# Attention FM on one core: a three-slot PSUM ring, longer bursts of one kind of matmul, paced gathers and a table copied by DMA

## The chip, the cores and the metric

One of the eight cores of a Trainium2 chip runs the kernel. The metric is the device time of one execution in microseconds. The three runs of the kernel before took 919.03, 920.51 and 921.53 us, median 920.51.

## What is computed

For 2048 samples of 32 fields, with a table of 12500 rows of 64 values:

```python
V = emb_v[x]                                   # 32 x 2048 x 64
iu, ju = np.triu_indices(32, k=1)              # the 496 pairs of fields
VV = V[iu] * V[ju]
hid = relu(einsum('pbk,kh->pbh', VV, at_w) + at_b)
score = einsum('pbh,ho->pbo', hid, at_h)
pooled = sum(VV * score, axis=0)
prob = sigmoid(pooled @ p + w0 + sum(w1[x], axis=0))
```

Everything is fp32.

## The kernel before, in words

The batch is worked off in 32 fills (`FILLS`) of 64 samples. A fill has two groups g of 16 samples side by side in columns, and two halves of the partitions, 64 embedding values each. A middle fill t goes through these stages.

Gather (GpSimd, L218 to L235): 16 indirect DMAs, each 128 rows of a table into `rows`. `rows` has two buffers; the first two fills read `emb_v` itself, later ones a joint table in HBM that holds the w1 value beside each row, once before it and once behind it, in two copies. The table is built at the start: SP loads `emb_v` and w1 (L191 to L195), VectorE and ScalarE copy them together (`join`, L329 and L380), SP stores four pieces (L202). Before each fill's gathers an index copy, `idx_stage` (L221), is made. GpSimd starts on fill t as soon as the rows of fill t-2 have been turned and their w1 values kept (L246, L247).

Turn (TensorE, L444 to L457): eight transposes of `rows` into the PSUM tile `TR`. ScalarE copies `TR` to `V` (L369) and, multiplied by p, to `pV` (L376), and the w1 values to `w1_all` (`w_all` in the profile, L392).

Products (VectorE, L336 to L351): 16 rounds a fill, one for each pair of step s (8 of them) and group g. A round is two tensor_tensor operations that write 1024 columns of pair products into one of eight slots of `X`.

Hidden (TensorE, L466 to L478): for each round four fp32 matmuls of 64x64 weights by 512 columns, which are eight matmul instructions in the profile, into `Z`, a ring of two slots of two PSUM banks each. ScalarE applies bias and ReLU to 1024 columns and writes one of eight slots of `H` (L424). TensorE waits at L471 for the ReLU of two rounds earlier.

Scores (TensorE, L488 to L501): `score_w` by `H`, 32-column weights in four column groups at a time, 16 matmul instructions a step, accumulated in `S`. `clear_scores` (L480 to L486) opens the accumulation with four bf16 matmuls on zeros.

Grams (TensorE, L503 to L520): for each of 16 samples and each g a matmul of 64-column weights from `pV` by 32 columns of `V` into `G`, so 64 matmul instructions a fill, in four quarters.

Pair sums (VectorE, L313 to L327): `gram` is `G` under a mask, `prod` is `S` times `gram`, `part` is its sum; done for fill t-1 in rounds 4 to 6 of fill t.

The order on TensorE is written out by hand in `products` (L528 to L546): after which of the 16 rounds scores, grams and turn come. It is, for one fill: rounds 0 and 1, scores of steps 6 and 7 of the fill before, rounds 2 and 3, a quarter of the grams, rounds 4 and 5, a quarter, rounds 6 and 7, clearing and scores of steps 0 and 1, round 8, turn of the next fill, round 9, scores of steps 2 and 3, rounds 10 and 11, a quarter, rounds 12 and 13, a quarter, rounds 14 and 15, scores of steps 4 and 5. The linear term (L548 to L561), 32 small matmuls, stands behind round 10 of the last fill. Fills 1 to 30 run in a hardware loop with two fills in its body.

## Time and profile before

| | us |
|---|---|
| three runs, median | 920.51 |
| the profiled execution, its own time | 918.6 |
| its span, from the first to the last instruction | 916.8 |
| TensorE busy | 866.9 |
| VectorE busy | 708.2 |
| ScalarE busy | 675.2 |
| GpSimd busy | 563.4 |

The profile is of one execution. The span is cut into instructions by line; "idle before" a group is time in which its engine had nothing to run, and what ended it. PE is TensorE's matmuls, PEld its weight loads, DVE VectorE, ACT ScalarE, POOL GpSimd, SP the queue of plain DMAs. The chain follows what ended last backwards through what each instruction waited for.

### The profile page before, as it was taken

The numbers are of one execution on the slowest core, as the hardware profiler recorded it, in microseconds if no ns is written. First come the engines' busy times: TensorE is split into PE (matmuls) and PEld (weight loads), VectorE is DVE, ScalarE is ACT, GpSimd is POOL, SyncE is SP. The second block draws the span as 40 slices with busy tenths as digits, with TensorE's granted clock in tenths as the row PEclk, the third lists the DMA queues.
The fourth block names the chain that finished last, engine by engine and source line by source line (L and its number), as shares of the span: only waits on it lengthen the run. The fifth ranks groups of instructions, "written<-read, shape, count | busy, mean of one in ns | idle before, by whom it ended". The sixth has DMA issues, their size and how long they took to land.

```text
span 916.8 us, 27050 instructions
## 1 busy us (share of the span) xinstructions
PE 866.9 (95%) x10676; PEld 339.1 (37%) x10676; DVE 708.2 (77%) x1179; ACT 675.2 (74%) x771; POOL 563.4 (61%) x584
## 2 busy tenths in 40 slices
PE   0549999999999999999999999999999999999998
PEld 0113333333433333333333333333333333333333
DVE  3555789777778977777898777779877777987772
ACT  3327777787877778787777788777778877777884
POOL 5717767555566765565676556556665555666770
PEclk9878999999999999999999999999999999999999
DMA  8972222222222222222222222222222222222000
GB/s 169 174 143 25 25 26 21 19 19 19 18 21 22 22 19 19 19 19 20 22 23 19 19 19 19 20 21 22 21 19 19 19 19 20 23 19 20 8 1 2
DMA packets 19638, 27.35 MB, mean 30 GB/s; under 512 B 10646, under 2 KB 10662, under 8 KB 18982
## 3 DMA queue, kind: packets, MB, share of 16 engines
q0 software_dynamic: 17408, 17.07, 25.0%
q1 hardware_dynamic: 1566, 10.02, 2.8%
q8 instruction: 11, 0.18, 0.1%
q10 hardware_dynamic: 648, 0.03, 0.0%
q14 instruction: 5, 0.04, 0.0%
HBM read 20.59 MB, written 6.51 MB: 30 GB/s over the span
## 4 chain that ended last, share of the span: by engine, by line
PE 92%; POOL 4%; DMA 2%; issue 1%; DVE 0%; SPq 0%; ACT 0%; POOLq 0%; DVEq 0%
PE Z L476 53%; PE S L497 26%; PE G L515 8%; PE TR L455 4%; POOL rows L233 3%; DMA rows<-in_L_rec_emb_v_dram,idx_stage 2%; PE S L485 1%; PE TR L556 0%; DMA idx_raw<-in_r_x_dram 0%; SPq L188 0%; ACT y_sb L439 0%; DVE prod L323 0%; DVE part L326 0%; POOL idx_stage L221 0%; PE TR L566 0%
## 5 line engine op out<-in xcount | busy, mean ns | idle before, releaser
L424 ACT ACTIVATE H<-Z,bias 128x1024 f32<-128x1024 f32 x512 | 546.5, 1112 | 192.2 <-PE Z L476 191.2
L348 DVE TENSOR_TENSOR X<-V 128x992 f32<-128x992 f32 (+15 forms) x1024 | 640.2, 696 | 24.2 <-ACT V L369 20.8
L233 POOL DMA_INDIRECT rows<-table,idx_stage x480 | 489.2, 1019 | 167.4 <-issue 144.5
L476 PE MATMUL Z<-X,w_sb 64*64 64x512 f32 x4096 | 517.2, 608 | 1.5 <-DVE X L348 1.2
L497 PE MATMUL S<-H,score_w 128*32 128x496 f32 (+15 forms) x4096 | 248.3, 383 | 0.0
L476 PEld LDWEIGHTS Z<-X,w_sb 64*64 64x64 f32 x4096 | 123.7, 131 | 182.4 <-issue 174.8
L497 PEld LDWEIGHTS S<-H,score_w 128*32 128x32 f32 x4096 | 111.2, 110 | 184.4 <-issue 139.8
L323 DVE TENSOR_TENSOR prod<-S,gram 128x512 f32<-128x512 f32 x32 | 22.1, 692 | 159.0 <-PE S L497 159.0
L515 PEld LDWEIGHTS G<-V,pV 128*64 128x64 f32 x2048 | 70.0, 137 | 103.8 <-issue 103.8
L221 POOL COPY idx_stage<-idx 128x16 uint32 (+1 forms) x32 | 7.1, 222 | 143.5 <-ACT w_all L392 122.6
L376 ACT ACTIVATE pV<-TR,pcol 64x512 f32<-64x512 f32 x128 | 87.0, 680 | 2.5
L515 PE MATMUL G<-V,pV 128*64 128x32 f32 x2048 | 84.3, 225 | 0.0
L455 PE MATMUL TR<-ident,rows 128*128 128x128 f32 x256 | 36.9, 289 | 44.6 <-DMA rows<-in_L_rec_emb_v_dram,idx_stage 44.6
L455 PEld LDWEIGHTS TR<-ident,rows 128*128 128x128 f32 x256 | 28.7, 146 | 70.6 <-issue 63.0
L369 ACT COPY V<-TR 128x512 f32<-128x512 f32 x64 | 34.2, 587 | 24.5 <-PE TR L455 24.5
L242 POOL DMA_INDIRECT w_all<-in_L_rec_w_dram,idx x32 | 33.5, 1048 | 9.8 <-issue 9.8
L233 POOL DMA_INDIRECT rows<-in_L_rec_emb_v_dram,idx_stage x32 | 32.7, 1023 | 10.8 <-issue 9.2
L317 DVE TENSOR_TENSOR gram<-G,upper 128x512 f32<-128x512 f32 x32 | 21.8, 681 | 8.1 <-PE G L515 8.1
L326 DVE TENSOR_REDUCE part<-prod 128x512 f32 (+1 forms) x32 | 21.8, 680 | 0.0
L485 PEld LDWEIGHTS S<-zeros 128*32 128x32 bf16 x128 | 3.3, 92 | 26.0 <-issue 26.0
L485 PE MATMUL S<-zeros 128*32 128x512 bf16 x128 | 12.8, 390 | 0.0
L392 ACT COPY w_all<-rows 128x8 f32 x60 | 9.3, 202 | 0.7
(38 smaller groups left out, 42.6 us busy)
## 6 DMA issues: line engine op xcount, KB each, us to landing
rows<-table,idx_stage POOLq DMA_INDIRECT x480
table<-joined SPq DMA_DIRECT2D x2, 1592.5 KB
table<-joined SPq DMA_DIRECT2D x2, 1560.0 KB
raw<-in_L_rec_emb_v_dram SPq DMA_DIRECT2D x1, 3104.0 KB, 11.7
rows<-in_L_rec_emb_v_dram,idx_stage POOLq DMA_INDIRECT x32, 12.3
w_all<-in_L_rec_w_dram,idx POOLq DMA_INDIRECT x32
idx_raw<-in_r_x_dram SPq DMA_DIRECT2D x4, 64.0 KB, 2.2
raw_w<-in_L_rec_w_dram SPq DMA_DIRECT2D x1, 48.5 KB, 13.4
```

What stands on the lines that cost most here:

```text
L233: pool.indirect_dma_start(out=rows[parity][:, g * FILL_M + m, half, c0:c1], out_offset=None, in_=source[half] if joint else source, in_off ...
L242: pool.indirect_dma_start(out=w1_all[:, Q, n:n + 1], out_offset=None, in_=w1, in_offset=at).then_inc(w1_first, 16)
L323: nc.vector.tensor_tensor(prod[:, :, :], S[:, :, :], gram[:, :, :], ALU.mult).then_inc(prod_ready, 1)
L348: last_one = nc.vector.tensor_tensor(xo, vj, vi.unsqueeze(3).to_broadcast(shape), ALU.mult)
L369: nc.scalar.copy(V[parity][:, g, :, :], TR[:, g, :].rearrange("p (b f) -> p b f", f=FIELDS)).then_inc(v_ready, 1)
L376: nc.scalar.activation(pV[parity][k, g, :, half, :, :], TR[k, g, :].rearrange("p (b i c) -> p b c i", c=2, i=FIELDS // 2), ACT.Copy, scale ...
L424: nc.scalar.activation(H[:, r % H_SLOTS, :, :], Z[:, r % Z_SLOTS, :, :], ACT.Relu, bias=bias[:, 0:1]).then_inc(hid_ready, 1)
L455: last = nc.tensor.transpose(TR[:, g, 128 * m:128 * m + 128], embs[:, g * FILL_M + m, 1:1 + 2 * EMB], ident[:, :])
L476: last = nc.tensor.matmul(Z[64 * par:64 * par + 64, r % Z_SLOTS, half, :], w_sb[k, :], X[k, r % X_SLOTS, par, :], start=True, stop=True)
L485: nc.tensor.matmul(S[32 * Q:32 * Q + 32, :, :], zeros[:, 0:32], zeros[:, :].rearrange("p (b j) -> p b j", j=FIELDS), start=True, stop=False)
L497: last = nc.tensor.matmul(S[at:at + 32, :, j0:FIELDS], score_w[:, slot, :], hid.rearrange("p (b j) -> p b j", j=nj), start=False, stop=(s ...
L515: last = nc.tensor.matmul(G[64 * g:64 * g + 64, b, :], pV[parity][:, g, b, :, :, :].rearrange("p h c i -> p (h c i)"), V[parity][:, g, b, ...
```

## The change

TensorE's order becomes four rounds and then scores, four times a fill. The turn of the next fill stands between the scores behind round 7 and round 8, all grams of the next fill behind the scores of round 15. Step and group now alternate in `ORDER`.

`Z` gets a third slot. `TR` is gone: the turn writes into the slot of the ring that would be next (`TURN_SLOT`), and the rounds behind it go on with the slot after it, so that rounds 8 and 9 wait for the ReLU of two rounds earlier and all others of three; round 10 waits for the copy of `V`. `S` and `G` are gone too: a tile `SG` for each parity holds the grams, which VectorE takes out under the mask, and then the scores, the first of which opens the accumulation; the clearing is dropped. A gram matmul of 64 columns becomes two of 32, in four column groups, 128 matmul instructions a fill. `pV` is one buffer, filled from `V` instead of `TR` with two masks of p, so its zeros need no memset. `V` is copied in one operation of 1024 columns.

GpSimd reads its indices straight from `idx`, or for the joint table from `joint_idx` (VectorE computes 66 times the index, plus 0 or 1), since there is now one table of 66 values a row, read from value 0 or 1 on as a flat list. Three fills read `emb_v` itself. The loop over fills is unrolled. The 16 gathers of a fill are in four groups of four, each released when TensorE has done a certain round: round 15 of the fill three before, and rounds 3, 7 and 11 of the fill two before. Of the 48 gathers of w1 one follows each fill, the rest come last.

SP loads `emb_v` only when the rows of fill 0 have landed, in 13 DMAs that write straight between the w1 columns; GpSimd writes those (`joined[:, :, :, c]`). `join` is gone. For the first fill the turn goes through `SG`. The linear term moves behind the last scores, in four row groups.

The diff, cut to what the text speaks of ("..." marks what is left out):

```diff
-ORDER = [(s, g) for four in (0, 4) for g in range(2) for s in range(four, four + 4)]
-SCORED_AFTER = {7: (0, 1), 9: (2, 3), 15: (4, 5)}
-LAST_STEPS, LAST_AFTER = (6, 7), 1
-GRAMS_AFTER = (3, 5, 11, 13)
-BATCHES = 4
-X_SLOTS, Z_SLOTS, H_SLOTS = 8, 2, 8
+ORDER = [(s, g) for s in range(STEPS) for g in range(2)]
+FIRST_ORDER = [(s, g) for g in range(2) for s in range(STEPS // 2)] + ORDER[ROUNDS // 2:]
+TURN_BEFORE = 8
+SCORED_AFTER = {3: (-1, (6, 7)), 7: (0, (0, 1)), 11: (0, (2, 3)), 15: (0, (4, 5))}
+LAST_STEPS = (6, 7)
...
+X_SLOTS, H_SLOTS, Z_SLOTS = 4, 4, 3
...
+JOINT = EMB + 2
+RUN = 8
+PLAIN_FILLS = 3
+PACE, PACED_FROM, PACED_EVERY = 2, 16, 4
...
+def z_slot(r):
+    return (r if r < TURN_BEFORE else r + 1) % Z_SLOTS
+TURN_SLOT = TURN_BEFORE % Z_SLOTS
+def z_before(r):
+    if r == 2:
+        return -3
+    if r < 2:
+        return r - 2
+    return r - 2 if TURN_BEFORE <= r < TURN_BEFORE + 2 else r - 3
...
-        S = ps("S", [128, GROUP, FIELDS])
-        G = ps("G", [128, GROUP, FIELDS])
-        TR = ps("TR", [128, 2, COLS])
-        logit = TR[0:QUARTERS, 0, :]
+        SG = [ps(f"SG{i}", [128, GROUP, FIELDS]) for i in range(2)]
...
+            for g in range(2):
+                sp.wait_ge(first_rows[g], 16 * GATHERS // 2)
+            sp.dma_start(tail[:, :, 1:1 + EMB], last_rows[0]).then_inc(tail_loaded, 16)
+            for k, (c0, c1) in enumerate(HALF_CHUNKS):
+                for c in range(c0, c1):
+                    sp.dma_start(joined[:, c, :, 1:1 + EMB], chunks(emb_v, c, c + 1)[:, 0, :, :]).then_inc(joined_loaded[k], 16)
+            sp.wait_ge(w1_joined, 4)
+            sp.wait_ge(tail_loaded, 16)
+            sp.dma_start(last_rows[1], tail[:, :, :]).then_inc(table_stored, 16)
+            for k, (c0, c1) in enumerate(HALF_CHUNKS):
+                sp.wait_ge(joined_loaded[k], 16 * (c1 - c0))
+                sp.dma_start(chunks(table, c0, c1), joined[:, c0:c1, :, :]).then_inc(table_stored, 16)
...
+            flat = table.rearrange("v (k o) -> (v k) o", o=1)
+            def gather(t, paced=False):
+                joint = t >= PLAIN_FILLS
+                source, at_rows = (flat, joint_idx) if joint else (emb_v, idx)
                 for g in range(2):
                     for m in range(FILL_M):
+                        if paced and m % PACE == 0:
+                            pool.wait_ge(z_ready, ROUNDS * (t - 3) + PACED_FROM + PACED_EVERY * (FILL_M * g + m) // PACE)
...
+            for half in range(2):
+                nc.gpsimd.memset(rows[0][:, :, half, W1_AT[half]], 0.0).then_inc(w1_cleared, 1)
+            pool.wait_ge(idx_ready, 1)
+            gather(0)
+            pool.wait_ge(w1_loaded, 32)
+            for c in (0, 1 + EMB):
+                nc.gpsimd.tensor_copy(joined[:, :, :, c], raw_w1[:, :, :]).then_inc(w1_joined, 1)
+                nc.gpsimd.tensor_copy(tail[:, :, c], tail_w1[:, :]).then_inc(w1_joined, 1)
+            pool.wait_ge(idx_ready, 2)
+            gather(1)
+            pool.wait_ge(first_turned, 2)
+            gather(2)
+            pool.wait_ge(rows_turned, 1)
+            pool.wait_ge(idx_ready, 4)
+            pool.wait_ge(table_stored, 16 * 3)
+            gather(3)
+            for t in range(4, FILLS):
+                pool.wait_ge(rows_turned, t - 2)
                 pool.wait_ge(w1_kept, 2 * (t - 3))
-                gather(t, parity, table)
-            pool.wait_ge(idx_ready, 1)
-            gather(0, 0, emb_v)
-            pool.wait_ge(idx_ready, 2)
-            gather(1, 1, emb_v)
-            pool.wait_ge(rows_turned, 2)
-            for half in range(2):
-                pool.wait_ge(table_stored[half], 16 * (1 + len(JOINS)))
-            gather(2, 0, table)
-            pool.wait_ge(rows_turned, 4)
-            gather(3, 1, table)
-            with pool.Fori(4, FILLS - 1, 2) as t:
-                refill(t, 0)
-                refill(t + 1, 1)
-            gather_w1(0)
-            gather_w1(1)
+                gather(t, paced=True)
+                gather_w1(1)
+            gather_w1(PLAIN_FILLS * GATHERS)
...
+            def mask_gram(t, parity):
+                dve.wait_ge(gram_ready, t + 1)
+                shape = [128, GROUP, FIELDS - 1]
+                nc.vector.tensor_tensor(gram[parity][:, :, 1:FIELDS], SG[parity][:, :, 1:FIELDS],
+                                        upper[:, 1:FIELDS].unsqueeze(1).to_broadcast(shape), ALU.mult
+                                        ).then_inc(gram_masked, 1)
+            def weigh(t, parity):
+                dve.wait_ge(gram_masked, t + 1)
+                dve.wait_ge(scored, STEPS * (t + 1))
+                nc.vector.tensor_tensor(prod[:, :, 1:FIELDS], SG[parity][:, :, 1:FIELDS], gram[parity][:, :, 1:FIELDS],
+                                        ALU.mult).then_inc(prod_ready, 1)
...
+                for r, (s, g) in enumerate(FIRST_ORDER if first else ORDER):
+                    if first and r in (0, STEPS // 2):
+                        dve.wait_ge(first_v, g + 1)
+                    if r == 8:
+                        mask_gram(t, parity)
+                    if r == 10 and not first:
+                        weigh(t - 1, 1 - parity)
+                    if r == 12 and not first:
+                        sum_pairs(t - 1)
+                    if not first:
+                        dve.wait_ge(z_ready, ROUNDS * t + r - 2 * X_SLOTS + 1)
...
+            def keep_v(t, parity):
+                act.wait_ge(rows_turned, t)
+                if not (isinstance(t, int) and t == 1):
                     act.wait_ge(x_ready, ROUNDS * (t - 1))
                     act.wait_ge(gram_ready, t - 1)
-                nc.scalar.copy(V[parity][:, g, :, :], TR[:, g, :].rearrange("p (b f) -> p b f", f=FIELDS)
+                nc.scalar.copy(V[parity][:, :, :], Z[:, TURN_SLOT, :, :].rearrange("p g (b f) -> p (g b) f", f=FIELDS)
                                ).then_inc(v_ready, 1)
-            def keep_pv(parity, g):
+            def keep_pv(t, parity, half):
+                if isinstance(t, int) and t == 0:
+                    act.wait_ge(first_v, 2)
+                    act.wait_ge(pmask_ready, 1)
+                else:
+                    act.wait_ge(v_ready, t)
+                    act.wait_ge(gram_ready, t)
...
+                nc.scalar.activation(pV[:, :, half, :, :], V[parity][:, :, :].rearrange("p b (i c) -> p b c i", c=2),
+                                     ACT.Copy, scale=pmask[:, half:half + 1]).then_inc(pv_ready, 1)
...
+                    if not last and not first:
+                        if r == 8:
+                            keep_v(t + 1, 1 - parity)
+                        if r == 10:
+                            keep_pv(t + 1, 1 - parity, 0)
+                        if r == 12:
+                            keep_w1(t + 1, 1 - parity)
+                        if r == 14:
+                            keep_pv(t + 1, 1 - parity, 1)
...
+                if r == TURN_BEFORE + 2 and not first and not last:
+                    pe.wait_ge(v_ready, t + 1)
+                elif not first or r >= Z_SLOTS:
+                    pe.wait_ge(hid_ready, ROUNDS * t + z_before(r) + 1)
...
+            def grams(t, parity):
+                pe.wait_ge(pv_ready, 2 * t + 2)
+                if not (isinstance(t, int) and t <= 1):
+                    pe.wait_ge(prod_ready, t - 1)
+                for b in range(GROUP):
                     for g in range(2):
-                        last = nc.tensor.matmul(G[64 * g:64 * g + 64, b, :],
-                                                pV[parity][:, g, b, :, :, :].rearrange("p h c i -> p (h c i)"),
-                                                V[parity][:, g, b, :], start=(b == 0), stop=(b == GROUP - 1),
-                                                skip_group_check=True)
+                        for half in range(2):
+                            at = 32 * (2 * g + half)
+                            last = nc.tensor.matmul(SG[parity][at:at + 32, b, :],
+                                                    pV[:, g * GROUP + b, half, :, :].rearrange("p c i -> p (c i)"),
+                                                    V[parity][:, g * GROUP + b, :], start=(b == 0), stop=(b == GROUP - 1),
+                                                    skip_group_check=True)
+                last.then_inc(gram_ready, 1)
...
+                    if r == TURN_BEFORE and not first and not last:
+                        pe.wait_ge(hid_ready, ROUNDS * t + TURN_BEFORE - Z_SLOTS + 1)
+                        turn(t + 1, 1 - parity)
+                    hidden(t, r, first, last)
                     if first and r == 3:
-                        turn(0, 0, (1,))
-                        keep_busy(8)
-                    if r == 8 and not last:
-                        pe.wait_ge(pv_ready, 4 * t + 4)
-                        turn(t + 1, 1 - parity)
+                        first_turn(1)
+                    if first and r == 5:
+                        grams(0, 0)
+                    if first and r == ROUNDS - 1:
+                        pe.wait_ge(hid_ready, ROUNDS - 2)
+                        turn(1, 1)
                     if r in SCORED_AFTER:
-                        if r == min(SCORED_AFTER):
-                            clear_scores(t, first)
-                        scores(t, SCORED_AFTER[r])
-                    if r == 10 and last:
-                        linear_term()
-                    if r == LAST_AFTER and not first:
-                        scores(t - 1, LAST_STEPS)
-                    if r in GRAMS_AFTER:
-                        grams(t, parity, first, r)
+                        back, steps = SCORED_AFTER[r]
+                        for s in steps:
+                            if back == 0:
+                                scores(t, parity, s)
+                            elif not first:
+                                scores(t - 1, 1 - parity, s)
+                    if r == ROUNDS - 1 and not last:
+                        grams(t + 1, 1 - parity)
...
+                for Q in range(QUARTERS):
+                    for q in range(QUARTERS):
+                        rng = slice(32 * q, 32 * q + 32)
+                        nc.tensor.matmul(logit[:, q, :], pick[rng, QUARTERS - 1 - Q:2 * QUARTERS - 1 - Q],
+                                         w1_all[rng, Q, :], start=(Q == 0), stop=False,
+                                         tile_position=(32 * q, 0), skip_group_check=True)
+            over_fills(pe, products)
+            for s in LAST_STEPS:
+                scores(FILLS - 1, (FILLS - 1) % 2, s)
+            linear_term()
```

## Rows read from the trace of the kernel before

**Rows 1.** The page, busy us by engine with share of the span and instructions.

```profile
PE 866.9 (95%) x10676; PEld 339.1 (37%) x10676; DVE 708.2 (77%) x1179; ACT 675.2 (74%) x771; POOL 563.4 (61%) x584
```

**Rows 2.** Windows: length, busy us (instructions) of PE, PEld, DVE, ACT, POOL, clock, DMA.

```profile
93.52:891.92 798.40, 798.40 (x9964) 311.72 (x9968) 649.91 (x1052) 625.24 (x721) 506.01 (x520) 1.00 0.24 19
```

**Rows 3.** The chain of waits through one fill: start us, length us, line, instructions.

```profile
522.44 1.02 PE TR L455 x8
523.46 1.02 PE Z L476 x8
524.48 1.86 PE S L497 x32
526.34 1.88 PE Z L476 x16
528.22 0.59 PE G L515 x16
...
538.89 2.07 PE Z L476 x16
...
545.94 0.33 PE S L485 x4
546.27 1.76 PE S L497 x32
```

**Rows 4.** Timeline of ScalarE and VectorE in that fill: start us, length us.

```profile
527.51 2.12 ACT L424 ACTIVATE H<-Z,bias 128x1024 f32<-128x1024 f32 x2 [1.83 <-PE Z L476]
...
534.50 2.80 ACT L376 ACTIVATE pV<-TR,pcol 64x512 f32<-64x512 f32 x4
537.32 0.31 ACT L392 COPY w_all<-rows 128x8 f32 x2
...
538.96 0.69 DVE L323 TENSOR_TENSOR prod<-S,gram 128x512 f32<-128x512 f32 x1 [4.96 <-PE S L497]
```

**Rows 5.** Timeline of TensorE's weight loads.

```profile
516.74 0.55 PEld L515 LDWEIGHTS G<-V,pV 128*64 128x64 f32 x16 [0.81 <-issue]
...
892.91 0.18 PEld L497 LDWEIGHTS S<-H,score_w 128*32 128x32 f32 x12 [0.30 <-issue]
```

**Rows 6.** The page: the gathers, two DMAs by their landing, the gathers' queue.

```profile
q0 software_dynamic: 17408, 17.07, 25.0%
...
L233 POOL DMA_INDIRECT rows<-table,idx_stage x480 | 489.2, 1019 | 167.4 <-issue 144.5
...
raw<-in_L_rec_emb_v_dram SPq DMA_DIRECT2D x1, 3104.0 KB, 11.7
...
rows<-in_L_rec_emb_v_dram,idx_stage POOLq DMA_INDIRECT x32, 12.3
```

**Rows 7.** Timeline of GpSimd at the head of a fill's gathers.

```profile
540.02 1.41 POOL L233 DMA_INDIRECT rows<-table,idx_stage  x1 [0.30 <-issue]
541.73 1.43 POOL L233 DMA_INDIRECT rows<-table,idx_stage  x1 [0.30 <-issue]
```

**Rows 8.** Timeline of the start.

```profile
24.84 1.09 PE L455 MATMUL TR<-ident,rows 128*128 128x128 f32 x4 [24.84 <-DMA rows<-in_L_rec_emb_v_dram,idx_stage]
...
28.91 4.95 DVE L348 TENSOR_TENSOR X<-V 128x992 f32<-128x992 f32 x8
...
41.81 1.12 PE L455 MATMUL TR<-ident,rows 128*128 128x128 f32 x4 [6.71 <-DMA rows<-in_L_rec_emb_v_dram,idx_stage]
```

**Rows 9.** The chain of waits through the start.

```profile
2.10 2.54 DMA idx_raw<-in_r_x_dram
...
48.47 18.83 DMA rows<-in_L_rec_emb_v_dram,idx_stage
...
96.63 1.02 PE TR L455 x8
```

**Rows 10.** The chain of waits through the end.

```profile
898.76 3.59 PE TR L556 x32
...
908.35 3.63 PE S L497 x64
```

331 lines of the change are left out of this document (136 added, 195 removed).

## The prediction

> **What bounds the kernel now.** I read the page's busy times first, then windows by stage, then the chain of waits through one fill, then the timelines of the loads, of ScalarE, VectorE and GpSimd, and last the two ends. TensorE is busy 95% of the span [rows 1]. The windows show where it is not: 798.40 us with TensorE busy throughout, between a start of 93.5 us and an end of 24.9 us (916.8 - 891.92) [rows 2]. The middle is 30 fills, 891.92 - 93.52 = 798.4, so 26.61 us each. There VectorE is busy 649.91 / 30 = 21.7 us a fill, ScalarE 625.24 / 30 = 20.8 and GpSimd 506.01 / 30 = 16.9, the issue ahead of its gathers not counted. Only work taken from TensorE's own line shortens the middle.
>
> One fill, from the chain [rows 3]: seven pairs of rounds at 1.88 us (13.16) and two single rounds at 1.02 (2.04), 0.37 of extra in three of the pairs, the longest 2.07, four S groups of two steps at 1.86 (7.44), the clearing 0.23 (0.33, less the 0.10 by which the S group behind it is shorter), four G quarters at 0.59 (2.36), TR 1.02. Sum 26.62. A round that continues a burst costs 1.88 - 1.02 = 0.86, one that begins a burst 1.02: each change to another kind of matmul and back costs 0.16 in Z alone. There are nine such excursions a fill.
>
> **The change, part by part, in a middle fill.**
> Rounds. The order of work becomes: four rounds, S, four rounds, S and TR, four rounds, S, four rounds, S and G. A burst of four is 1.02 + 3 x 0.86 = 3.60, four of them 14.40, against 15.20 + 0.37: -1.17. The 0.37 goes if the third slot removes the wait for ScalarE. Check: ScalarE does a ReLU every 1.01 us inside a pair (two in 2.12, each 1.11) [rows 4], slower than 0.86, so it falls behind in a burst and catches up under S. Over rounds 8 to 15 TensorE has 1.02 + 3.60 + 1.86 + 3.60 + 1.86 + 1.25 = 13.2 us. ScalarE has 8 x 1.01, one V copy of 1024 columns (as a ReLU, 1.11), two pV copies of 1024 columns (0.68 for 512 now; 1.2 each taken, bounds 1.11 and 1.36) and 0.3 for w_all: 11.9 [rows 4]. Laid out in order, the first ReLU 1.24 us behind the start of its round, each round finds its slot free; the closest is round 15, which needs the ReLU of round 12, about 0.2 us earlier. Round 10 needs the V copy, 0.5 us early. So nothing is charged, and what is late next is that round 15.
> Clearing: -0.23. S stays 7.44.
> G. 64 matmul instructions with 64-column weights, two column groups at a time, become 128 with 32-column weights, four at a time. Now 16 loads take 0.55, one 0.14, so a pair follows a pair after (0.55 - 0.14) / 7 = 0.059. In S, which loads the 32-column form that G will have, twelve loads (three fours, with only 16 columns moving in the ones between) lie within 0.18, one taking 0.11: (0.18 - 0.11) / 2 = 0.035 from four to four [rows 5]. 32 fours x 0.035 + 0.13 for the change of mode = 1.25, against 2.36: -1.11. Bounds: below, the loads inside a four are some 0.01 apart in all, which leaves 0.030, and no change of mode behind S: 1.0. Above, every instruction keeps today's share, 0.59 / 16 = 0.037, 128 x 0.037 = 4.7. I take the S rows, which have the same shape.
> TR stays 1.02; it now sits directly behind S.
> Sum: 14.40 + 7.44 + 1.02 + 1.25 = 24.11 us a fill, 2.51 less.
>
> **What the others need in 24.11.** VectorE: the same products, three pair operations of 31/32 the size: 21.7. Its wait for S before prod, 4.96 us [rows 4], shrinks to about 2.4, and its products stay up to eight rounds ahead. The gram mask waits for the G at the end of the fill before; VectorE gets there within 0.3 us of it. ScalarE: 20.5. GpSimd: 17 gathers (16 and one of w1) at 1.02 [rows 6] and 0.31 of issue [rows 7] = 22.6; the idx_stage copy goes. The groups are released four rounds apart (6.0 us for 4 x 1.33 = 5.3) and the last one is due 13 rounds after its release, so the rows are there in time. Nobody waits for a paced gather; what is queued behind the pacing wait is only the next gather.
>
> **The start.** Now the first rows are turned at 24.84, the second half at 41.81 [rows 8], fill 1's at 67.3, fill 2's at 96.63 [rows 9]. Fill 1's gathers were issued from 28.6 to 48.5 and the last landed 18.83 us later, beside table loads and stores. After: gathers start about 1 us earlier (the copy at L221 and the issue behind it go); eight at 1.25 end at 15.6, and with no table on the queues landing is 2.5 us, as for idx_raw [rows 9]; turned at 18. The second eight: 25.6, turned at 28. GpSimd's line then sets much: w1 copies about 1, gather(1) to 47.9, gather(2) to 69.1, gather(3) to 90. Moving the table behind the first rows puts its 3.1 MB load into 28 to 50 or so and its store behind it. Bounds: the plain load landed in 11.7 us [rows 6]; by the gathers' cost, 25.0% of 16 x 916.8 us over 544 gathers of 128 rows, nearly all of 256 or 260 bytes, 0.053 us a row, 12500 rows take 41. At 25 the table is stored by 69, when gather(3) wants it. On SP's queue the loads, one per chunk, stand behind the wait for the first rows; behind them is only the output. The joins leave VectorE and ScalarE, which the first products waited behind (28.91 against a turn at 24.84 [rows 8]).
> Fill 1's rows land 2.5 to 12.3 us after 47.9 [rows 6, 9]; I take 7: 55. Then TR 1.02, V 1.11, pV 2.4, G 1.25, and 2 x 3.60 + 2 x 1.86: 16.7, so fill 2 is turned at 71.7. GpSimd allows 69.1 + 2.5 = 71.6. With 12.3 it is 77. I take 74, against 96.63 now. That is 22.6 us.
>
> **The end.** From the turn point of the last fill: 2 x 3.60 + 3 x 1.86 = 12.8, then 4.8 as now (912.0 to 916.8) [rows 10]. The linear term, 3.59 of the chain now, stands behind the last S and beside 1.4 us of VectorE (prod at 0.69 [rows 4] and its sum, as long); in four row groups it is 0.9 (bound 3.59, then 2.2 us show). Its remaining 20 w1 gathers, 25 us, have about 45 us.
>
> **Sum.** 74 + 30 x 24.11 + 12.8 + 4.8 = 814.9 of span. The profiled execution took 918.6 at a span of 916.8: +1.8 = 816.7. The median of 920.51 is 1.9 above it: 818.6, so **818 us**.
>
> **Rivals.**
> A. *G does not run four wide.* With pairs at 0.059, 64 x 0.059 + 0.13 = 3.9 a fill, +2.65 x 30: 898. For: no row has more than twelve such loads in a row, and the 128 now come in one block. Against: the S rows. 0.07. By the upper bound, 4.7 and 922, nothing is gained: 0.02.
> The Trainium skill (TensorE: Matmul & The Clock Gate, "Wait — 56ns, not 53.3ns?") says that the starts of matmuls never come closer than about 25 ns; by that G would be 128 x 0.025 = 3.2 us and the kernel about 876 (an estimate from the page). Twelve loads of S within 0.18 us, each 0.11 long and followed by its matmul, speak against it here.
> B. *GpSimd becomes the bound, and the kernel is slower.* Place: the gathers at L233. At the head of each batch two or three are slow, 1.41 and 1.43 in place of 0.94, while VectorE runs [rows 7]; these two start 1.71 apart. If four short groups a fill and a denser VectorE make all of them like that, 17 x 1.71 = 29.1 us a fill: 74 + 872 + 17.6 + 3.7 = 967. It binds from 24.11 / 17 = 1.42 and turns slower than before from 1.62. Against: a GpSimd that is late does not pause, and the mean with only one pause a fill is 1.33. 0.05. Half of them slow, 1.52: 25.8, 871: 0.05.
> The Trainium skill (SBUF — State Buffer, "Who interferes with whom") says that a VectorE instruction with two SBUF inputs contends with GpSimd's SBUF reads. The slow gathers fit that, the many at 0.94 beside the same products do not.
> C. *ScalarE paces the second half.* If V and pV push rounds 9 to 15 to 1.01 instead of 0.86 a round: 0.9 a fill, 845. 0.07. This is also the case in which the third slot does nothing.
> D. *The table is late.* At 41 us of load gather(3) starts at 83 and fill 3's turn waits 10 to 20 us: 834. 0.08.
> The forecast: 0.66.
>
> **How the numbers follow.** 803 is the forecast with fills of 23.9 (G at its lower bound, no mode change between S and G) and fill 2 turned at 71; 850 takes in C and D. A and B stand outside, 0.19. Faster by over 0.3% (what a measurement of this kernel tells from no change) is everything but the upper bound of A and the slow end of B: 0.93; same 0.02; slower 0.05.
>
> **What would show it.** Bursts of four rounds of 3.60 with no 0.1 to 0.2 added; no clearing; G near 1.25 in one piece; fills of 24.1; 1.33 us from gather to gather; the turn of fill 2 near 74. It is wrong if TensorE shows waits for gathers in the middle, if G is over 2.4, or if the fill is over 25.

## The result and the profile after

The changed kernel takes 867.53 us (865.84 to 868.82), the kernel before beside it 920.78 us: a ratio of 0.9423, 95% interval 0.94 to 0.9447. The forecast was 818, the range 803 to 850. It is faster, as said, but by half of what was said, and outside the range. The profiled execution has a span of 864.8 us against a forecast of 814.9, so there are 49.9 us to find. Of the loops over fills only GpSimd's is unrolled; the other engines keep a hardware loop with two fills in its body, which matters below.

First the page's busy times, queues and groups of instructions.

```profile
PE 804.1 (93%) x12600; PEld 348.1 (40%) x12600; DVE 700.3 (81%) x1175; ACT 642.8 (74%) x672; POOL 608.3 (70%) x574
...
q0 software_dynamic: 17920, 17.08, 40.5%
...
L559 PE MATMUL SG<-V,pV 128*32 128x32 f32 x4096 | 58.3, 200 | 11.5 <-issue 7.5
```

Windows of the changed kernel, with the columns of [rows 2]: from the turn of fill 4 to that of fill 31, and a stretch of the start.

```profile
149.34:822.02 672.68, 664.42 (x10593) 288.88 (x10585) 584.94 (x946) 540.14 (x567) 506.90 (x463) 1.00 0.41 21
...
58.00:82.00 24.00, 15.55 (x251) 7.51 (x252) 15.58 (x25) 8.92 (x9) 9.05 (x9) 0.79 0.83 66
```

The middle is 27 fills in 672.68 us, 24.91 each, where [rows 2] give 26.61 and the forecast said 24.11: 27 x 0.80 = 21.7 us of the 49.9. The turns of fills 2, 3 and 4 stand at 90.74, 122.41 and 149.34 in the trace, the forecast had 74, 98.1 and 122.2: 27.1 us. From the last turn to the end it is 42.78 where 24.11 + 12.8 + 4.8 = 41.7 were forecast: 1.1 us. The three make 49.9.

The chain through one fill, as in [rows 3]:

```profile
473.20 1.02 PE Z L493 x8
474.23 3.59 PE Z L529 x32
477.82 1.86 PE SG L544 x32
479.68 3.59 PE Z L529 x32
483.28 1.86 PE SG L544 x32
485.14 1.20 PE SG L559 x72
486.34 0.08 issue
486.42 0.39 PE SG L559 x10
486.81 0.42 issue
487.23 3.67 PE Z L529 x32
```

Bursts of four take 3.59 (forecast 3.60), but the one behind the grams 3.67, S 1.86, the turn 1.02, the clearing is gone, and nothing waits for ScalarE. One term is far off: from the first gram matmul to the next round it is 487.23 - 485.14 = 2.09 us, not 1.25. A part of that has no releaser ("issue"): no engine and no DMA that the profile shows ended it.

The timeline of the start: SP's loads and stores of the table, TensorE in fill 1, the gather that waited for the table, and the turn of fill 3:

```profile
31.21 50.84 SPq L228 DMA_DIRECT2D joined<-in_L_rec_emb_v_dram  x12
...
58.03 1.94 PE L493 MATMUL Z<-ident,rows 128*128 128x128 f32 x8 [5.07 <-DMA rows<-in_L_rec_emb_v_dram,idx]
...
72.15 0.75 PE L559 MATMUL SG<-V,pV 128*32 128x32 f32 x35 [7.47 <-issue]
...
82.65 4.71 SPq L234 DMA_DIRECT2D table<-joined  x2
...
85.31 3.60 PE L529 MATMUL Z<-X,w_sb 64*64 64x512 f32 x13 [3.15 <-issue]
...
96.78 2.03 POOL L262 DMA_INDIRECT rows<-table,joint_idx  x1 [27.30 <-DMA table<-joined]
...
122.41 1.94 PE L493 MATMUL Z<-ident,rows 128*128 128x128 f32 x8 [6.93 <-DMA rows<-table,joint_idx]
```

Of the 16.7 us by which fill 2 is turned late, 3.0 come before the turn of fill 1 (58.03 against 55), 10.6 are two stops without an instruction inside fill 1, and 3.1 are left over, in a stretch where the matmuls run at a lower clock (granted 0.79 in 58 to 82; the turn takes 1.94 in place of 1.09). Fill 3 is then another 7.6 later: SP needs 50.8 us to issue twelve loads of the table, so the table is stored at 96 (forecast 69), GpSimd waits 27.3 us for it, and the turn 6.9. The last 2.8 come up to the turn of fill 4: 0.8 are those of a middle fill, and behind the wait the turn takes 1.94 and the first burst 4.62, at a granted clock of 0.92 in 122 to 149, which is another 1.9.

### The profile page after: what moved, and what is told of

It reads as the page before. It is cut to its first block, busy times and chain, and to the rows that moved or that the text cites. A ratio compares the mean times of both kernels' runs of the same rounds, so it can differ in the third digit from the quotient of the medians.

```text
span 864.8 us, 30490 instructions
## 1 busy us (share of the span) xinstructions
PE 804.1 (93%) x12600; PEld 348.1 (40%) x12600; DVE 700.3 (81%) x1175; ACT 642.8 (74%) x672; POOL 608.3 (70%) x574
## 3 DMA queue, kind: packets, MB, share of 16 engines
q0 software_dynamic: 17920, 17.08, 40.5%
## 4 chain that ended last, share of the span: by engine, by line
PE 85%; SPq 5%; DMA 4%; POOL 4%; issue 2%; ACT 0%; DVE 0%; POOLq 0%
PE Z L529 49%; PE SG L544 26%; PE SG L559 5%; SPq L228 5%; POOL rows L262 4%; PE Z L493 4%; DMA joined<-in_L_rec_emb_v_dram 1%; DMA table<-joined 1%; DMA rows<-in_L_rec_emb_v_dram,idx 1%; DMA rows<-table,joint_idx 0%; DMA idx_raw<-in_r_x_dram 0%; PE Z L614 0%; SPq L214 0%; PE Z L602 0%; SPq L225 0%
## 5 line engine op out<-in xcount | busy, mean ns | idle before, releaser
L262 POOL DMA_INDIRECT rows<-table,joint_idx x464 | 510.7, 1101 | 193.1 <-issue 122.8
L529 PE MATMUL Z<-X,w_sb 64*64 64x512 f32 x4096 | 476.1, 601 | 11.4 <-issue 8.3
L544 PE MATMUL SG<-H,score_w 128*32 128x496 f32 (+15 forms) x4096 | 249.3, 383 | 1.0 <-issue 1.0
L544 PEld LDWEIGHTS SG<-H,score_w 128*32 128x32 f32 x4096 | 109.8, 110 | 206.4 <-issue 111.8
L421 ACT ACTIVATE pV<-V,pmask 128x1024 f32<-128x1024 f32 x64 | 80.8, 1266 | 0.1
L410 ACT COPY V<-Z 128x1024 f32<-128x1024 f32 x31 | 31.4, 1013 | 51.6 <-PE Z L493 51.6
L559 PE MATMUL SG<-V,pV 128*32 128x32 f32 x4096 | 58.3, 200 | 11.5 <-issue 7.5
L262 POOL DMA_INDIRECT rows<-in_L_rec_emb_v_dram,idx x48 | 48.8, 1017 | 18.0 <-issue 14.2
L559 PEld LDWEIGHTS SG<-V,pV 128*32 128x32 f32 x4096 | 51.2, 109 | 21.9 <-issue 16.8
L493 PE MATMUL Z<-ident,rows 128*128 128x128 f32 x248 | 35.6, 289 | 12.0 <-DMA rows<-table,joint_idx 6.9
L493 PEld LDWEIGHTS Z<-ident,rows 128*128 128x128 f32 x248 | 28.0, 146 | 14.8 <-issue 12.9
## 6 DMA issues: line engine op xcount, KB each, us to landing
joined<-in_L_rec_emb_v_dram SPq DMA_DIRECT2D x12, 256.0 KB, 16.7
```

Source lines behind the costliest of these rows:

```text
L262: pool.indirect_dma_start(out=rows[t % 2][:, g * FILL_M + m, half, c0:c1], out_offset=None, in_=source, in_offset=bass.IndirectOffsetOnAxi ...
L410: nc.scalar.copy(V[parity][:, :, :], Z[:, TURN_SLOT, :, :].rearrange("p g (b f) -> p (g b) f", f=FIELDS)).then_inc(v_ready, 1)
L421: nc.scalar.activation(pV[:, :, half, :, :], V[parity][:, :, :].rearrange("p b (i c) -> p b c i", c=2), ACT.Copy, scale=pmask[:, half:half ...
L493: last = nc.tensor.transpose(Z[:, TURN_SLOT, g, 128 * m:128 * m + 128], embs[:, g * FILL_M + m, 1:1 + 2 * EMB], ident[:, :])
L529: done = nc.tensor.matmul(Z[64 * par:64 * par + 64, z_slot(r), half, :], w_sb[k, :], X[k, s % X_SLOTS, par, COLS * g:COLS * g + COLS], sta ...
L544: last = nc.tensor.matmul(SG[parity][at:at + 32, :, j0:FIELDS], score_w[:, slot, :], hid.rearrange("p (b j) -> p b j", j=nj), start=(s == ...
```

## Experiments

On three occasions every kernel took a half longer or more, the kernel before too (1377 to 1418 us), with TensorE stopped again and again and no releaser named (in the run without pacing 328 stops of 0.3 to 8.6 us behind 200 us). A chip on which the kernel before took 1418 gave 918 in a later run, so it is not the chip alone, and nothing is compared across. Those occasions are told together at the end. All the others had the kernel before at 917.5 to 918.6 us, and the changed kernel once more at 863.38 (ratio 0.9407, interval 0.9391 to 0.9423), turns at 87.05, 118.49 and 145.83:

> The changed kernel itself, unaltered, beside the kernel before on whatever chip this is. On the chip of the four runs so far the kernel before took 1418 us in place of 921, with stops at TensorE that the trace puts down to no one (0.65 to 2.8 us each inside the block of gram matmuls). Theory C (that chip feeds instructions to TensorE more slowly; nothing in the kernels changed): on a chip where the kernel before takes 921, this one takes 867 again; on one where it takes about 1418, this one is slowed as well, by more than the kernel before if its block of 256 instructions is the most sensitive part, to over 1370. Rival: the kernels of the last call were slow for a reason of their own.

### The grams in two halves between pieces of S

```diff
+                            mixed = r == ROUNDS - 1 and not last
+                            if mixed and s == steps[-1]:
+                                grams(t + 1, 1 - parity, 0, GROUP // 2)
+                                scores(t, parity, s, (GROUP // 2, GROUP))
...
-                    if r == ROUNDS - 1 and not last:
-                        grams(t + 1, 1 - parity)
```

`scores` with that last argument issues the other half of the grams between its two segments, so the order is 64 gram matmuls, 8 of the last step of S, 64 of grams, the last 8 of S.

> The kernel of e1_mixed again, so that it stands beside the changed kernel on the same chip. Theory Q (queue runs dry in the gram block): where the kernel before takes 921, about 845, a fill 24.1 us in place of 24.9. Rival W (the array itself): 867.

Measured 844.57, ratio 0.9223 (0.9185 to 0.926), 18.8 us less than the changed kernel; fills of 24.26. The chain:

```profile
470.82 1.00 PE SG L544 x16
471.82 0.63 PE SG L563 x48
472.45 0.58 PE SG L544 x7
473.03 0.56 PE SG L563 x44
473.59 0.34 PE SG L544 x8
473.92 0.18 issue
474.10 3.66 PE Z L529 x32
```

Each half takes 0.56 to 0.63 us, and none of the halves between 149 and 822 us has a pause of more than 0.1 us between two starts; the last two steps of S take 1.92 us in sum, 1.86 before. The rate of the forecast's S rows holds, and rival W falls: the array takes such matmuls at that rate. What theory Q says beyond that, that TensorE runs out of instructions, is the reading that fits stops without a releaser; no row shows the instruction queue.

The traces add a condition. In the changed kernel's own middle 23 of the 27 blocks of 128 have two or three pauses of 0.16 to 0.28 us between starts, 0.62 us a fill on the mean of all 27, and four have none. A block with stops and, below it, one without, each with the gathers beside it:

```profile
235.93 0.94 POOL L262 DMA_INDIRECT rows<-table,joint_idx  x1 [0.30 <-issue]
235.97 2.13 PE L559 MATMUL SG<-V,pV 128*32 128x32 f32 x128
...
247.77 14.67 DVE L395 TENSOR_TENSOR X<-V 128x608 f32<-128x608 f32 x24
252.62 0.95 POOL L262 DMA_INDIRECT rows<-table,joint_idx  x1 [0.30 <-issue]
...
256.20 7.05 POOL L262 DMA_INDIRECT rows<-table,joint_idx  x1 [0.30 <-issue]
261.33 1.30 PE L559 MATMUL SG<-V,pV 128*32 128x32 f32 x128
```

All four blocks without a stop stand under one gather that takes 7.05 or 7.06 us. The seven other traces of this time with a block of 128 agree: 22 more blocks in their middles are free of stops, each under one long gather (5.2 to 7.1 us), and so is the block at 86.77 in the run with few rows, under its gather of 14.76. Behind the last gather of all there are two blocks, at 831.62 without pacing and at 931.68 with two slots, and neither has a stop. In every one of the 187 middle blocks with stops a gather starts within the block or at most 0.05 us ahead of it. So in these traces the stops need both, the long block and a gather that starts beside it; how a gather holds TensorE's instructions up is not shown.

### The table loaded by two DMAs

```diff
-                for c in range(c0, c1):
-                    sp.dma_start(joined[:, c, :, 1:1 + EMB], chunks(emb_v, c, c + 1)[:, 0, :, :]).then_inc(joined_loaded[k], 16)
+                sp.dma_start(raw[:, c0:c1, :, :].rearrange("p c r k -> p c (r k)"),
+                             emb_v[0:MAIN, :].rearrange("(c p r) k -> p c (r k)", p=128, r=RUN)[:, c0:c1, :]
+                             ).then_inc(joined_loaded[k], 16)
...
+                nc.scalar.copy(joined[:, c0:c1, :, 1:1 + EMB], raw[:, c0:c1, :, :]).then_inc(emb_joined, 1)
```

> The kernel of e2_table again, beside the changed kernel on the same chip. Theory D (the twelve DMAs of 256-byte runs cost the start): where the kernel before takes 921, about 847, fill 3 turned near 102 us in place of 122.4. Rival P (GpSimd's line of gathers sets it): over 859.

Measured 856.16, ratio 0.9356 (0.9293 to 0.9419); SP's side:

```profile
30.31 4.29 SPq L229 DMA_DIRECT2D raw<-in_L_rec_emb_v_dram  x2
...
51.71 7.82 SPq L237 DMA_DIRECT2D table<-joined  x2
```

The issue, 47 us in the changed kernel beside it, is 4.3, and fills 3 and 4 are turned at 114.6 and 139.8 in place of 118.5 and 145.8. But fill 2 is still turned at 89.95, and TensorE's stops in fill 1 are still there (3.22 and 6.99 us at 67.67 and 84.71). So the long issue cost the wait of fill 3 and not the stops; the expected 847 had counted them as gone. The time lies between theory D's and rival P's, the interval overlaps that of the changed kernel (0.9391 to 0.9423), and one of the four executions took 865.7, so the 7 us rest on the other three (853.4 to 856.7) and on the turns.

### Both

> Both edits together, gram halves between the pieces of the last score step and the table by two plain DMAs and two ScalarE copies. If Q and D both hold they touch different stretches and add: where the kernel before takes 921, about 825, close to the 818 that was predicted for the change itself. If one of them falls, it gives what the other gives alone.

Measured 839.44, ratio 0.9136 (0.9112 to 0.916): the best that was seen beside a kernel before of 918, and 2.8% better than the change. It misses the expected 825, since the stops in fill 1 stay (turns 91.48, 116.19, 140.64).

### No pacing

```diff
-                gather(t, paced=True)
+                gather(t)
```

> The changed kernel without the pacing waits: the sixteen gathers of a fill follow one another as soon as the rows of the fill two before are turned. Second time of this edit: on the chip of its first time the kernel before took 1418 us and every second gram block took some 22 us, so that what it says of a chip where the kernel before takes 920 is open. Theory N (pacing does nothing for the time, since nobody waits for a gather in the middle, and the stops in the gram block have nothing to do with the gathers): 860 to 868, fill 24.9. Rival G (bursts of gathers on the DMA queues hold up the fetch of TensorE's instructions, and pacing keeps them apart): over 875, with gram blocks longer than the 1.74 to 2.58 us of the changed kernel.

Measured 863.18, ratio 0.9399 (0.9376 to 0.9422), fills of 24.90, gram blocks as in the changed kernel. The release of the gathers by rounds is worth nothing here: theory N.

### A ring of two slots

```diff
-X_SLOTS, H_SLOTS, Z_SLOTS = 4, 4, 3
+X_SLOTS, H_SLOTS, Z_SLOTS = 4, 4, 2
...
+        TR = ps("TR", [128, 2, COLS])
```

The turn goes to `TR`, and every round waits for the ReLU of two rounds before.

> The changed kernel with a ring of two slots and a PSUM tile of its own for the turn, all else as it is; second time of this edit, for the same reason. Theory R (the third slot is what makes the bursts of four cost 3.59: with two, a round inside a burst waits for ScalarE, which gives a slot back every 1.01 us instead of 0.86): bursts of four 3.9 to 4.3, fill 26 to 28, 900 to 960. Rival O (the longer bursts alone do it, as ScalarE kept up in the pairs before): bursts 3.6 to 3.7, at most 880.

Measured 966.71, ratio 1.0525 (1.0507 to 1.0542). A burst in the chain:

```profile
491.52 1.88 PE Z L522 x16
493.40 0.50 issue
493.90 2.10 PE Z L522 x16
495.99 1.86 PE SG L537 x32
```

A burst of four is 4.47 us in place of 3.59: 0.50 stopped in the middle and 0.39 inside the second pair (2.10 against 3.59 - 1.88) (the profile calls this wait "issue" too, but only the slots and the turn's own tile differ). Four bursts make 3.5 us, and the fill is 28.51, 3.6 more. It is theory R, a little beyond its own bounds: without the third slot the longer bursts would have made the kernel 5% slower than before. To this order of work the slot is worth 103 us (966.71 - 863.38).

### The stops in fill 1: where do they come from?

The trace of the changed kernel has instruction DMAs of 16 KB: ten between 40 and 141 us, while fills 0 to 3 go by, and then none till 838. So what they bring, code of the loop, is fetched in its first pass only. One started at 69.83 and took 1.07 us, one at 82.78 and took 1.14; TensorE's two stops end 1.2 and 1.4 us behind the ends of these, which is why I take them for its code. The other traces bear it out: in the nine of this time in which all rows are fetched, TensorE has 18 stops of over 2 us without a releaser before 160 us, and each ends 1.2 to 1.6 us behind the end of such a DMA. Three runs asked what delays them.

First the store of the table was put behind fill 1 (kernel of both repairs, fill 3 also from the plain table):

```diff
-PLAIN_FILLS = 3
+PLAIN_FILLS = 4
...
             sp.wait_ge(tail_loaded, 16)
+            sp.wait_ge(z_ready, 2 * ROUNDS)
```

> The kernel with gram halves between score pieces and the table loaded by two DMAs (839.44 us), and now the table is stored only when the rounds of fill 1 are done, while fill 3's rows too come from the plain table (64 w1 gathers, one or two after each fill). Theory D (the stops of 3.2 and 7.0 us in fill 1, where TensorE has no instructions, come from instruction DMAs that wait behind the table's store, 3.2 MB beside the gathers): both stops are under 1 us in sum, fill 2 is turned by 84 (now 91.5), and as fill 3 no longer waits for the table it is turned by 109 (116.2): 824 to 833. Rival C (the stops belong to the first pass through the loop's code, which is long and fetched for the first time there, or to the gathers of fill 2): they stay at 7 to 11 us in fill 1, fill 3 turned near 115, 834 to 842.

Measured 844.09, ratio 0.9214 (0.9161 to 0.9266). Theory D falls, rival C's stops of 7 to 11 us in sum stay, and fill 3 is turned at 119.23:

```profile
71.44 0.58 PE L577 MATMUL SG<-V,pV 128*32 128x32 f32 x26 [5.12 <-issue]
...
87.75 3.68 PE L543 MATMUL Z<-X,w_sb 64*64 64x512 f32 x13 [5.34 <-issue]
```
```profile
58.00:82.00 24.00, 16.32 (x251) 7.61 (x252) 15.48 (x25) 9.83 (x10) 18.51 (x19) 0.72 0.86 24
```

The store is not their cause: without it the DMA share in 58 to 82 us is still 0.86, at 24 GB/s. That is the gathers of fill 2.

Then the gathers of fill 2 were cut to 8 rows each, all else as in the change (and, in the other run, with the late store and fill 3 cut too):

```diff
-                            pool.indirect_dma_start(out=rows[t % 2][:, g * FILL_M + m, half, c0:c1], out_offset=None,
+                            n = 8 if t in (2,) else 128
+                            pool.indirect_dma_start(out=rows[t % 2][0:n, g * FILL_M + m, half, c0:c1], out_offset=None,
                                                     in_=source,
-                                                    in_offset=bass.IndirectOffsetOnAxis(ap=at_rows[:, col:col + 1], axis=0)
+                                                    in_offset=bass.IndirectOffsetOnAxis(ap=at_rows[0:n, col:col + 1], axis=0)
```

> The changed kernel, but the sixteen gathers of fill 2 fetch 8 rows each in place of 128, so that the results of fill 2 are made of old rows; the table's load and store stay. Theory F (TensorE's code for fills 1 and 2 is fetched once, by 16 KB DMAs, and these wait behind the gathers of fill 2 on the DMA engines): the stops in the gram block and in the second burst of fill 1, 7.5 and 3.2 us, fall to under 2 us in sum, and the DMA share of 58 to 82 us falls well below 0.83. Rival S (they wait behind the table's load and store): the stops stay at 8 to 11 us here. Rival C (the fetch is late by itself, whatever else moves): 8 to 11 us here and in the next run too.

> The kernel of the late store (844.09 us), but the gathers of fills 2 and 3 fetch 8 rows each in place of 128: while TensorE goes through fill 1 there is neither table nor gather traffic to speak of. Theory F and rival S: the stops of 5.7 and 7.7 us in fill 1 are gone, under 1.5 us in sum. Rival C: they stay at 8 us or more in sum.

Measured 861.34 us (ratio 0.9388, 0.9361 to 0.9416) for the first; the second took 839.86 and 827.18 in its two executions, and only its stops are read (the stops of the late store, which its expectation gives as 5.7 and 7.7 us, are the 5.12 and 5.34 above). The first, TensorE in fill 1:

```profile
61.65 2.19 PE L560 MATMUL SG<-V,pV 128*32 128x32 f32 x128 [0.95 <-ACT pV L422]
63.99 3.66 PE L530 MATMUL Z<-X,w_sb 64*64 64x512 f32 x32 [0.15 <-issue]
...
69.45 3.66 PE L530 MATMUL Z<-X,w_sb 64*64 64x512 f32 x32
...
74.94 1.09 PE L494 MATMUL Z<-ident,rows 128*128 128x128 f32 x8
```
```profile
58.00:82.00 24.00, 22.69 (x369) 9.93 (x372) 22.70 (x38) 17.48 (x17) 14.40 (x9) 0.97 0.54 169
```

Theory F. The stops are gone while 3.9 MB of table go by (169 GB/s in all), and fill 2 is turned at 74.94, where the forecast had 74. What delays the instructions is the gathers, though they move a seventh of the bytes per us. (In the second run TensorE has no stop above 0.1 us without a releaser in 56 to 82 either.) The late store had no table traffic in that stretch and kept its stops, so the table is neither needed nor enough for them. The 16 KB DMA that started at 69.83 in the changed kernel started at 58.52 here. Whether it is the gathers' rows, their length in the engines or their place in a queue is not shown. The clock follows: granted 0.79 with the stops, 0.97 without.

### One gather of 14.8 us

Yet that run was hardly faster (861.34 against 863.38), since fill 3 was turned only at 114.99. Its chain goes along GpSimd:

```profile
73.41 2.61 POOL rows L263
76.02 0.30 issue
76.32 14.76 POOL rows L263
```

VectorE's timeline there:

```profile
75.67 14.58 DVE L396 TENSOR_TENSOR X<-V 128x608 f32<-128x608 f32 x24
90.17 0.66 DVE L357 TENSOR_TENSOR gram<-SG,upper 128x496 f32<-128x496 f32 x1
```

One gather began 0.65 us behind the start of 24 products in a row, each with two inputs in SBUF, and ended 0.9 us after VectorE had gone on to the gram mask, which reads PSUM. In the next run VectorE may be four rounds ahead instead of eight:

```diff
-                        dve.wait_ge(z_ready, ROUNDS * t + r - 2 * X_SLOTS + 1)
+                        dve.wait_ge(z_ready, ROUNDS * t + r - X_SLOTS + 1)
```

> The run with few rows in fill 2 (861.34 us), and VectorE's products may be four rounds ahead of TensorE in place of eight, so that VectorE pauses more often. There, one gather of fill 3 took 14.76 us (from 76.32) beside a stretch of 14.58 us (from 75.67) in which VectorE ran products without a pause, and two more 2.61 and 2.67. Theory V (a gather's work on GpSimd goes on only when VectorE pauses): no gather takes over 5 us, the sixteen of fill 3 end by 100 instead of 112, and fill 3 is turned by 103 instead of 115. Rival T (the gather waited for something on the table's or the gathers' DMA queue): a gather of over 10 us stays near 76, and fill 3 is turned near 115. The middle may become slower in both cases, where TensorE then waits for products.

Measured 841.67, ratio 0.9166 (0.9139 to 0.9192), against 0.9388 without. The timeline of GpSimd:

```profile
74.77 2.01 POOL L263 DMA_INDIRECT rows<-table,joint_idx  x1 [8.01 <-DMA table<-joined]
```

No gather takes over 2.1 us, fill 3 is turned at 100.93 (forecast 98.1), and the middle has fills of 24.87, so the shorter lead costs nothing. Of the 20.4 us of span, 14.1 are there by the turn of fill 3, 2.9 more by that of fill 4, and 3.4 come in the middle. Rival T falls. Theory V holds for this gather, but as it is worded ("goes on only when VectorE pauses") it says too much. The changed kernel has 28 stretches of 24 products without a pause, and in four of them one gather is held, for 7.05 or 7.06 us. The one at 256.20 (shown with the halves above) ends at 263.25, 0.8 us behind the end of the stretch that began at 247.77; the one at 252.62 began inside the same stretch and took 0.95. The other 294 gathers that start in the 28 stretches take 0.94 to 1.43. With the shorter lead there is no stretch of 24 and, in its four traces, no gather over 2.6 us. What decides which gather is held is open. The Trainium skill (SBUF — State Buffer, "Who interferes with whom") says that a VectorE instruction with two SBUF inputs contends with GpSimd's SBUF reads; the held gathers agree, the many at 0.94 beside the same products don't follow from it.

### The table's loads before the first rows

```diff
-            for g in range(2):
-                sp.wait_ge(first_rows[g], 16 * GATHERS // 2)
```

> The changed kernel with one wait taken out: SP issues the table's loads from the start, not when the rows of fill 0 have landed. Issue of the twelve DMAs stays at some 50 us, so they end near 60 in place of 82 and the table is stored by 75 in place of 96. Theory P (the place of the load sets fill 3's turn, and its traffic at the start costs the first rows only a little): first turn at 20 to 25, fill 3's rows wait for GpSimd's line alone, so fill 3 is turned 5 to 12 us earlier than 118 to 122: 853 to 862. Rival Q (the loads in front of the first gathers hold up the first rows by as much as they save): first turn 28 or later, 863 to 880.

Measured 867.32, ratio 0.9472 (0.9423 to 0.9522), which meets the changed kernel's. First turn at 23.10 (19.71 in the change), second at 36.61 (30.34), fill 2's at 101.04, fill 3's at 126.87. Theory P fails, and the time is rival Q's (863 to 880), though not by a first turn of 28 or later: put first, the table is in the way of the first rows, and the longest stop in fill 1 was 13.65 us. The issue of the twelve loads took 33.5 us, so it too depends on what else moves: 50.8 in the change, 27.9 with few rows. Whether SP is slow at such loads itself or waits for room behind them is not shown.

### On the slow occasions

Beside a kernel before of 1417.72: halves of grams 0.9569, two-DMA table 0.9441, no pacing 1.0429, two slots 1.035.

> The changed kernel with the 128 gram matmuls of the next fill cut in two halves of 64 that stand between the pieces of the last score step (scores of step 4, half the grams, first piece of step 5, the other half, second piece of step 5) and no longer in one block with nothing behind it. Theory Q (the queue ahead of TensorE runs dry in the block: 8 instructions are used up every 0.035 us, the stops of 0.17 to 0.28 us and the 0.24 to 0.63 us from the last gram matmul to the next round are the instruction supply showing through): the stops and the long step to the next round go, a fill falls from 24.9 to about 24.1 us, the kernel by 27 x 0.8 = 22 us, to about 845. Rival W (32-column weights in four column groups cost that time in the array itself, wherever they stand): a fill stays at 24.9, the kernel at 867.

> The changed kernel with the table loaded as two plain DMAs with runs of 2 KB into a tile of its own, and two ScalarE copies of 3072 columns (about 2.8 us each) into the joint tile, in place of twelve DMAs with runs of 256 bytes straight into it. Theory D (the start is lost to these twelve DMAs: SP needs 50.8 us to issue them, the table is stored at 96 in place of 69 us, and with the DMA engines full the instructions for TensorE arrive late, 7.5 and 3.2 us without an instruction): issue falls under 2 us, the table is stored by about 70, the two stops shrink to under 1 us together, fill 2 is turned near 77 in place of 90.7 and fill 3 near 102 in place of 122.4; the kernel falls by about 20 us, to 847. Rival P (GpSimd's own line of gathers, 16 after 16, sets the start, whoever loads the table): fill 3 is turned no earlier than 115, the kernel falls by under 8 us.

> The changed kernel without the four waits per fill that hold back the groups of gathers; a fill's 16 gathers start when the rows of the fill two before are turned and their w1 kept. Theory N (the pacing holds nobody up and saves nobody anything, since TensorE never waits for rows in the middle): same time within 0.3%. Rival G (paced groups cost GpSimd its slow restarts, or the bursts of gathers disturb others): over 3 us one way or the other, and TensorE's waits for rows or VectorE's product times differ.

> The changed kernel with a ring of two slots and the turn in a tile of its own, as before; the bursts of four rounds stay. Theory R (with bursts of four the third slot is what keeps TensorE from ScalarE's pace: the third round of a burst would wait for the ReLU of the first, which ends 2.35 us behind the burst's start where the third round could start at 1.77): 0.5 to 0.7 us a burst, 2 to 2.8 us a fill, the kernel 60 to 85 us slower, 930 to 950, slower than the kernel before. Rival O (the order of the work alone brings the gain, the third slot only the 0.37 us a fill of waits that the kernel before showed): at most 12 us slower, 880.

Beside 1377.43 and 1386.13 two edits were run that ask whether VectorE's hold of GpSimd costs the start also where all rows are fetched:

> All that helped in one kernel, with every row fetched: gram halves between score pieces, the table loaded by two DMAs (839.44 us together), and VectorE's products at most four rounds ahead. Theory V (VectorE's unbroken products also hold the gathers of fills 2 and 3 where all rows are fetched): fill 3 is turned by 112 in place of 116.2, the middle stays at 24.3: 831 to 837. Rival N (in this start VectorE is often stopped anyway, because TensorE has stops of its own, and the gathers take 20.6 us for sixteen as they should): fill 3 turned at 115 to 117, 837 to 842, no difference to 839.44.

> The changed kernel with that one edit alone, VectorE at most four rounds ahead. Theory V: 855 to 861. Rival N: 861 to 868, as the changed kernel, with fill 3 turned at 118 to 122; the middle stays at 24.9 in both.

> The kernel with all three repairs a second time, since the first time fell on a chip where the kernel before took 1377 us. On a chip where it takes some 918: theory V (VectorE holds the gathers in this start as well): fill 3 turned by 112, middle at 24.3, 831 to 837, a ratio to the kernel before of 0.905 to 0.912. Rival N (it makes no difference here): 837 to 842, a ratio of 0.912 to 0.917 like the 0.9136 without this edit.

The kernel with all three repairs took 1256.16 (1236.58 to 1298.06; ratio 0.9006, 0.8919 to 0.9093) and, the second time, 1251.75 (1227.99 to 1270.74; no ratio), the one with the shorter lead alone 1277.17 (0.9245, 0.9183 to 0.9308). Their middles are 36.5 to 38.5 us a fill, with stops all through, so the question stays open. What stops TensorE on such an occasion also stays open; pacing, worth nothing where the kernel before takes 918, may matter there (1.0429), but the unchanged kernel was not run beside it.

## Why the prediction was wrong

**The bound and the middle: right, but for one term.** The bound was TensorE's own line; bursts, S, the turn, the clearing and the third slot's freedom from ScalarE came out within 0.01 us each, except that the burst behind the grams took 3.67 where 3.60 was forecast and the S ahead of the turn 1.90. Rival C did not occur, and the run with two slots shows how near it was: it is the slot that keeps it away.

**G: the term that was mis-sized.** It was taken as 1.25 between bounds of 1.0 and 4.7, and the fill shown has 2.09; a fill took 24.91 - 24.11 = 0.80 more than forecast, nearly all of it here. The rate from the S rows [rows 5] was right: a block without a stop, here in the run with few rows,

```profile
86.77 1.30 PE L560 MATMUL SG<-V,pV 128*32 128x32 f32 x128
```

has its 128 starts within 1.11 us, 0.035 from four to four. The rule of the Trainium skill (TensorE: Matmul & The Clock Gate, "Wait — 56ns, not 53.3ns?") that was weighed there, starts no closer than some 25 ns, would make it 3.2 us (an estimate from the page); the trace disagrees, with 8.7 ns from start to start on the mean. What the step left out is the sentence in rival A itself, that no row had more than twelve such loads in a row. The trace has two things in its place: the pauses inside the block, 0.62 us a fill, which come only beside gathers, and the step from the last gram matmul to the next round, taken as 0.13. It is 0.24 in most fills that are the first in the loop's body and 0.61 to 0.65 in most that are the second, where TensorE's code goes back to the head of the loop; 0.39 on the mean. The run with halves takes away 0.65 a fill, which are the pauses, and leaves the step.

**The start: three costs that no row of before had shown.** "Fill 1's rows landed 55": 58.03, near. "Fill 2 turned at 74": the mechanism lacked 10.6 us in two stops, and without them, in the run with few rows, it was 74.94. That is in part luck: the steps from rows to turn, summed to 16.7, took 18.75 there (56.19 to 74.94), and the 2.3 us that had been put on top of the sum of 71.7 made up for it. In the changed kernel they took 32.7, so beside the stops 3.3 more, in the stretch with the lower clock. The forecast put the supply of instructions at nothing and gave no reason; in the kernel before TensorE waited for rows from 54.4 to 67.4, so no row of it had shown this. "Table stored by 69": 96, because the forecast took the load's cost from its bytes and rows (bounds of 11.7 and 41 us) and left out its issue by SP, 50.8 us for rows cut into 256-byte runs and 4.3 for the same bytes in two plain loads. Rival D had the mechanism, a turn that waits 10 to 20 us, and gave it 0.08; it was 6.9 at the turn itself, since fill 2 was late too. And "gather(3) to 90" left out that a gather can be held beside VectorE's products; that cost nothing in the changed kernel's start, where GpSimd waited for the table, and was seen once fill 2 was early.

**What the others need: right.** GpSimd was no bound (mean of a gather 1.10 us, [rows 6] have 1.02), rival B did not occur. That pacing costs nothing was right; that it gains nothing, either, the run without it shows.

**The range** took its width from G and from C and D, one at a time. G and D both went the bad way at once, and the stops were outside every case. Its lower end does not come out of its own terms either: 818 - 30 x (24.11 - 23.9) - 3 is 808.7, not 803.

## What to carry to other kernels

A block of 128 very short matmuls beside indirect gathers lost 0.62 us a fill in stops; cut into blocks of 64 (the one other size tried) with longer matmuls between, it lost none, 18.8 us for moving lines. In the first pass through a loop's code look at what else is on the DMA engines, above all gathers: TensorE's stops there went when the gathers' rows did. With four rounds in a burst the third slot of the ring was worth 103 us. An engine that runs far ahead without a pause can, now and then, hold a gather of GpSimd for as long as it runs; a shorter lead cost nothing, and helped by 20 us where that gather was on the path. Whether it helps where all rows are fetched is open.

## What the hardware showed unasked

Two things are shown and not explained. The gathers' queue was busy 40.5% of the span for 17.08 MB, and 36.8% when the same kernel ran once more, where before the same bytes took 25.0% [rows 6]; with a ring of two slots, at 28.51 us a fill, it was 26.4%. The lead has no part in it: with few rows the DMA share of the middle was 0.31, and 0.29 with few rows and the short lead. And on some occasions the same kernels take a half longer, with stops of TensorE all through.
